# First attention: the cosine products of the rotation move from GpSimd to VectorE

## The reference

```python
qkv = x @ w_qkv.T                      # 16 query heads, 4 key heads, 4 value heads of 128, and a gate
q = _layernorm(q, q_norm_w, q_norm_b)  # over the 128 numbers of each head
k = _layernorm(k, k_norm_w, k_norm_b)
q = _rope(q, cos, sin)                 # out = [xr*c - xi*s, xr*s + xi*c]
k = _rope(k, cos, sin)
scores = einsum('bhqd,bhkd->bhqk', q, k) / sqrt(D)
attn = softmax(where(causal, scores, -inf), axis=-1)
out = einsum('bhqk,bhkd->bhqd', attn, v)
out = out * sigmoid(gate)
return out @ w_o.T
```

## Time and profile before

| what | us |
|---|---|
| three runs: median (lowest to highest) | 868.32 (867.44 to 869.45) |
| the profiled execution, whole | 867.89 |
| its span, first to last instruction | 866.2 |
| PE busy in the span | 706.4 (82%) |
| DVE busy | 576.8 (67%) |
| ACT busy | 322.8 (37%) |
| POOL busy | 306.4 (35%) |

### The profile page before, as it was taken

How to read it: one execution, slowest core, us unless ns; L and a number is a source line. 1 busy time by engine, 2 the same in 40 slices (tenths; PEclk the granted TensorE clock), 3 DMA queues, 4 the chain that set the end, 5 groups by cost and what they waited for, 6 DMA issues and landing times.

```text
span 866.2 us, 12266 instructions
## 1 busy us (share of the span) xinstructions
PE 706.4 (82%) x4097; PEld 443.0 (51%) x4114; DVE 576.8 (67%) x1797; ACT 322.8 (37%) x880; POOL 306.4 (35%) x364
## 2 busy tenths in 40 slices
PE   4579999999999999899998859727788986949960
PEld 2345555555555555567785434424455554524540
DVE  5768888888888888634115958355788853785543
ACT  1335555555555555533002224002466553214200
POOL 2432333333332223200002352673465422236274
PEclk9779999999999999999997969877899999888995
DMA  7000000010000000000198023230000005004243
GB/s 289 0 1 35 3 1 25 1 37 0 25 1 0 1 25 1 0 1 1 63 408 293 1 74 121 81 95 21 0 2 1 2 1 220 24 2 140 83 125 91
DMA packets 18686, 49.77 MB, mean 57 GB/s; under 512 B 4032, under 2 KB 12992, under 8 KB 18112
## 3 DMA queue, kind: packets, MB, share of 16 engines
q1 hardware_dynamic: 13728, 35.75, 11.0%
q0 software_dynamic: 4896, 13.24, 5.3%
HBM read 41.32 MB, written 7.34 MB: 56 GB/s over the span
## 4 chain that ended last, share of the span: by engine, by line
PE 30%; DVE 30%; POOL 17%; issue 10%; ACT 7%; DMA 5%; POOLq 0%; SPq 0%; ACTq 0%; DVEq 0%
PE ps L1234 6%; POOL ma L465 6%; ACT nq L619 5%; POOL xg L588 4%; POOL hrs L471 4%; DVE ps L787 4%; DVE probs L929 4%; DVE prod L1110 3%; PE ps L1526 3%; DVE hst L874 3%; PE ps L1443 2%; DVE qT L885 2%; DVE oT L939 2%; PE ps L1576 2%; DMA y_rows<-turn 2%
## 5 line engine op out<-in xcount | busy, mean ns | idle before, releaser
L787 DVE CUSTOM_DVE_ANT_0 ps<-ps,maskb 128x512 f32<-128x512 f32 (+3 forms) x256 | 119.3, 518 | 64.2 <-PE ps L1255 49.0
L1220 PE MATMUL ps<-w_qkv_a,xnT 128*128 128x512 f32 (+1 forms) x256 | 98.9, 515 | 11.2 <-ACT nq L619 10.5
L471 POOL TENSOR_TENSOR hrs<-hve,half 128x5 f32<-128x5 f32 x32 | 38.6, 1206 | 159.1 <-DVE hneg L900 159.0
L654 ACT COPY pT<-ps 128x512 f32<-128x512 f32 (+1 forms) x96 | 43.2, 523 | 121.2 <-PE ps L1335 121.2
L619 ACT ACTIVATE nq<-ps,hnm,hrs 128x128 f32<-128x128 f32 x160 | 59.4, 459 | 69.2 <-POOL hnm L473 69.2
L588 POOL DMA_INDIRECT xg<-y_rows,slot_of x64 | 64.8, 1012 | 55.2 <-DMA y_rows<-turn 36.4
L465 POOL TENSOR_TENSOR ma<-nq,rotA 128x512 f32<-128x512 f32 x32 | 54.4, 1701 | 65.5 <-ACT nq L619 65.5
L1255 PE MATMUL ps<-kT,qT 128*128 128x512 f32 (+3 forms) x256 | 76.6, 443 | 1.0 <-DVE qT L885 1.0
L1267 PE MATMUL ps<-pT,vA 128*128 128x512 f32 (+3 forms) x256 | 74.2, 433 | 0.0
L635 ACT ACTIVATE probs<-ps,negmax 128x512 f32<-128x512 f32 (+3 forms) x128 | 66.6, 559 | 9.3 <-DVE negmax L787 8.7
L1172 DVE SCALAR_TENSOR_TENSOR x_res<-xg,share,x_res 128x256 f32<-128x256 f32 x64 | 31.3, 489 | 51.5 <-DMA xg<-y_rows,slot_of 49.8
(11 more groups left out here) (175 smaller groups left out, 1422.0 us busy)
## 6 DMA issues: line engine op xcount, KB each, us to landing
w_down<-in_w_down SPq DMA_DIRECT2D x2, 4096.0 KB, 13.2
y_rows<-turn SPq DMA_DIRECT2D x32, 128.0 KB
w_qkv_a<-in_w_qkv SPq DMA_DIRECT2D x4, 768.0 KB, 5.1
w_gate<-in_w_gate SPq DMA_DIRECT2D x4, 512.0 KB, 3.2
w_o<-in_w_o SPq DMA_DIRECT2D x1, 2048.0 KB, 13.1
xn_rows<-xn SPq DMA_DIRECT2D x2, 1024.0 KB, 9.8
x_res<-in_x SPq DMA_DIRECT2D x2, 512.0 KB, 6.1
xg<-y_rows,slot_of POOLq DMA_INDIRECT x64, 2.8
```

Of the source, the lines that this page charges most:

```text
L471: pool.tensor_tensor(hrs[:], hve[:], half[:, 0:REP + 1], ALU.pow).then_inc(head_pow, 1)
L787: return dve.tensor_tensor_reduce(out=scores, in0=scores, in1=maskb[:, S - (i4 + 1) * P:], scale=-1.0, scalar=HUGE, op0=ALU.add, op1=ALU.m ...
L1220: mm = pe.matmul(dst, xnT[:, k, col:col + P], w, start=(k == 0), stop=(k == KT - 1))
```

## The change

The two products with the cosine table leave GpSimd's step and are written into VectorE's, between the two products with the sine table and the addition. They keep their shapes, their operands and their semaphore. GpSimd keeps the power and the product behind it. The order of GpSimd's instructions alone had kept it from overwriting `hrs` and `hnm` before ScalarE had read them; now a wait on `norm_done` in front of the power does.

```diff
@@ pool, step @@
-                if 1 <= r <= TILES:
-
-                    n = (r - 1) % ST
-                    pool.wait_ge(norm_done, s * (REP + 1))
-                    if r >= 2:
-                        pool.wait_ge(rope_done, s - 1)
-                    pool.tensor_tensor(ma[:, 0:REP], nq[:, 0:REP], rotA[:, 0, n:n + 1].broadcast_to([P, REP, HD]),
-                                       ALU.mult).then_inc(rotA_done, 1)
-                    pool.tensor_tensor(ma[:, REP], nq[:, REP], rotA[:, 1, n], ALU.mult).then_inc(rotA_done, 1)
                 if r < TILES:
 
                     pool.wait_ge(st_done, 2 * (s + 1))
+                    if r >= 1:
+                        pool.wait_ge(norm_done, s * (REP + 1))
                     pool.tensor_tensor(hrs[:], hve[:], half[:, 0:REP + 1], ALU.pow).then_inc(head_pow, 1)
@@ dve, step, rotated @@
                     dve.tensor_tensor(plain(mb[:, REP:J]), swapped(nq[:, REP:J]), plain(rotB[:, 1, n:n + 1]),
                                       ALU.mult).then_inc(rotB_done, 1)
+                    if r >= 2:
+                        dve.wait_ge(rope_done, s - 1)
+                    dve.tensor_tensor(ma[:, 0:REP], nq[:, 0:REP], rotA[:, 0, n:n + 1].broadcast_to([P, REP, HD]),
+                                      ALU.mult).then_inc(rotA_done, 1)
+                    dve.tensor_tensor(ma[:, REP], nq[:, REP], rotA[:, 1, n], ALU.mult).then_inc(rotA_done, 1)
                     dve.wait_ge(rotA_done, s * 2)
                     dve.wait_ge(rotB_done, s * 2)
```

## The result

| kernel | runs | median us (lowest to highest) | ratio to before, 95% interval |
|---|---|---|---|
| before, beside the first comparison | 4 | 868.07 (867.44 to 869.45) | |
| with the change | 4 | 853.81 (848.92 to 856.61) | 0.9835 [0.9813, 0.9856] |
| before, beside the second comparison | 9 | 867.90 (865.80 to 870.19) | |
| with the change, again | 5 | 855.31 (854.16 to 856.68) | 0.9854 [0.9835, 0.9873] |

The change makes the kernel 14.3 us faster in the first comparison and 12.6 in the second. The forecast was 855.9, 12.4 less than before. All nine executions lie between 848.9 and 856.7.

The account below looks back on a forecast made before the run. No engine is full; a loop through VectorE, GpSimd and ScalarE sets the 11.19 us step. Full steps gain 14.0 us, the filling loses 1.6: 12.4 off the median 868.32 gives 855.9 us, range 852.5 to 860.0.

Parts of the forecast that it names:

- Full step: Steps 6 to 32: sine product to addition falls from 2.31 to 1.79 us, gaining 0.52; step 11.19 to 10.67.
- The exponentials' lid: VectorE's reciprocal also needs ScalarE's exponentials, so a full step can gain at most 0.52 to 0.55 us.
- Collision: GpSimd and VectorE, reading `nq` together, hold each other up; the small sine product is stretched by 1.08 us.
- rival (c): Small sine product slow by itself in full steps; step row 0.56 us longer, about 885 us; chance 0.03.
- 27 steps: All full steps, r = 6 to 32, at 0.52 us each: 14.0 us gained.
- Filling: Steps before r = 6: moved products are new VectorE work, 0.80 us each in steps 4 and 5; 1.6 lost.
- the up to 2 us on top: Filling steps 2 to 4: extra loss if GpSimd's power had to wait for VectorE's whole rotation.
- Rival (a): Reciprocal waits for exponentials or a dearer product, 0.10 to 0.17 us a step; about 859.5 us; chance 0.18.
- Rival (b): TensorE keeps its clock in step 32, or step 5's scores run faster; 854 us; chance 0.14.
- Rival (d): Another loop through TensorE takes over at once: nothing gained, filling paid; 870 us; chance 0.03.
- Signs of being wrong: Reciprocal waits for ScalarE, power's median rises above 1.17 us, or stages behind 369 us change their length.
- TensorE's lid: Full steps: from 0.71 us of waiting, TensorE could not do a step below 10.48 us.

Follow-up runs that it names:

- GpSimd's unread products: The changed kernel, but GpSimd still makes both cosine products every step, into a tile that no instruction reads; 893.30 us in one run.
- the late gating: The changed kernel with VectorE's gating of a head's output put behind the next tile's moments in steps 6 to 31; 842.89 us, ratio 0.9709.

## Why the prediction was right, and where it was not

- *Full step.* Forecast 10.67, measured 10.66. The three first pitches were right (0.61, 0.20, 0.60 for 0.60, 0.20, 0.60). The fourth was 0.32 and not 0.39, so the addition came at 1.73 and not 1.79. The exponentials' lid, which the forecast put at 0.52 to 0.55, took 0.05 of that back, and 0.53 was left. That the two nearly cancel is luck; that no more than 0.55 could come out was read rightly from the earlier trace rows, and leaving out a product showed that it is a lid.
- *Collision.* The reading of the 1.36 us as GpSimd's doing was an inference from step 5. GpSimd's unread products showed it, and with it rival (c) fell: the small product is not slow by itself. Moving the small product alone showed that the stretch stays when the wait of 0.35 is gone. That both engines read the same `nq`, as the prediction put it, is not needed for it: the rows of the filling below show the like with no tile in common.
- *27 steps.* 26 distances gave 13.9 and 13.7 us and the last step half a microsecond, so 14.4 and 14.2 together: 14.0 forecast.
- *Filling.* 1.6 forecast; 1.0 and 1.7 in the two traces by the stages, 1.2 and 1.9 by GpSimd's share of it put back. The steps shared it as said: 0.74 each in 4 and 5 (the addition at 1.73 against 0.99). One part of the mechanism was not foreseen: not the power but the small product behind it is held, for the whole addition. GpSimd's row begins 0.06 behind VectorE's and ends 0.06 behind its end:

```profile
36.15 1.53 POOL L464 TENSOR_TENSOR hrs<-hve,half 128x5 f32<-128x5 f32 x1 [7.16 <-DVE hneg L898]
...
36.58 0.29 DVE L855 TENSOR_TENSOR mb<-nq,rotB 128x128 f32<-128x128 f32 x1
36.78 0.68 DVE L859 TENSOR_TENSOR ma<-nq,rotA 128x512 f32<-128x512 f32 x1
...
37.39 0.28 DVE L861 TENSOR_TENSOR ma<-nq,rotA 128x128 f32<-128x128 f32 x1
...
37.70 0.82 DVE L864 TENSOR_TENSOR mb<-ma,mb 128x640 f32<-128x640 f32 x1
37.76 0.82 POOL L466 TENSOR_TENSOR hnm<-hneg,hrs 128x5 f32<-128x5 f32 x1
```

  It takes 0.20 in a full step. The power is 1.53 to 1.54 as it was the earlier trace rows, 0.37 longer than in a full step: that is less than the length of one large product of VectorE's, and not the run of them, and the up to 2 us on top did not come. The other way round nothing was held: VectorE's three products beside the power are 0.29, 0.68 and 0.28 long, as in a full step. What the Trainium skill ("SBUF — State Buffer", section "Who interferes with whom") says against the change is thus half borne out: GpSimd's small product waits for VectorE's addition, but the power, though it began first, did not keep VectorE's products out for its 1.53; here the measurement decides.
- *Rival (a)* was half there: the exponentials are the later half of the tie, but by 0.05 (0.79 for 0.74 from the addition to the reciprocal) and not by 0.10 to 0.17. *Rival (b)* came true in one trace and not in the other; two traces do not show whether the change makes it likelier. *Rival (d)* fell by the step.
- *Signs of being wrong.* In the full steps the reciprocal's line shows no idle time before it; its 4 waits of 4.6 us in all lie behind step 32 and were there before (4.7 us). The power's median is 1.17 as before. The stages behind the last gating changed by 3.9 us in the first trace, most of it by the clock of the router's projection, and by 0.1 in the second.
- *TensorE's lid.* This step failed. From 0.71 us of waiting I concluded that TensorE cannot do a step below 10.48. It does one in 10.25. The row of a group of matmuls is longer than the distance from its start to what follows it without a wait. Here is the projection ahead of the transposes, 1.88 long before the change and with the late gating; first before:

```profile
191.00 1.88 PE L1220 MATMUL ps<-w_qkv_a,xnT 128*128 128x512 f32 x4
```

  Then with the late gating:

```profile
193.44 1.88 PE L1222 MATMUL ps<-w_qkv_a,xnT 128*128 128x512 f32 x4
...
195.16 0.60 PE L1284 MATMUL ps<-ident,mb 128*128 128x128 f32 x4
```

  With the late gating the transposes start 1.72 behind it. Before, they started 2.59 behind it (193.59 in the earlier trace rows), so TensorE lost 0.87 there and not 0.71: idle time that a view shows is a lower bound of the slack. That gives 11.19 - 0.87 = 10.32; most of the rest is the transposes themselves, with 0.55 to the next projection with the late gating and 0.60 before. In the forecast the error cost nothing, since the exponentials ended the gain first; in the expectation for the late gating it was some 7 us (850 for 842.9).
- *GpSimd's busy time* fell by 63.7 us and not by some 70. The products were 70.6 (54.4 and 16.2); 1.9 came back in the held small products, 4.3 in products of the shared expert, which are longer in this one trace (25.0 us; 20.7 before and 20.3 in the second trace).
- *Behind the rotation* the forecast expected the clock of step 32 to fall; it did so in the second trace. The median of the nine executions, 854.5, is 1.4 under the forecast. Where these 1.4 lie is open, since only two of the nine have a trace: the fastest, which gained 6.0 us behind step 32, where its clock stayed up, and one of 856.1, which gained 0.5 there.

## What to carry to other kernels

Where an elementwise product is split over GpSimd and VectorE and both read SBUF at the same time, look at the longest of each engine's instances beside the shortest: a 128x128 product that takes 1.36 us here and 0.28 there may be paying for its neighbour, and giving all of it to VectorE can be faster than sharing. Then ask what ends last next: here the gain stopped at the exponentials, and a product that was taken away besides brought nothing. Before trusting an engine's idle time as its lid, measure the distance from start to start where nothing waits, or move something off the loop and see. Work that belongs to neither end of a loop is worth trying elsewhere: the gating, moved, gave another 0.41 us a step (10.66 to 10.25).

## What the runs showed of the hardware that I had not expected

- A GpSimd product of 128x5, 0.20 us by itself, was 0.82 long behind a VectorE addition of 128x640 with two SBUF inputs that had begun 0.06 earlier: it ended only 0.06 behind it.
- The collision goes both ways in turns: with two products on each engine, GpSimd's became 1.78 and 0.50 (1.26 and 0.46 alone), VectorE's 1.36 and 0.94 (0.28 and 0.68 alone).
- After the same idle times TensorE's clock fell in one execution and not in another (2.40 against 1.31 us for ten transposes). The Trainium skill, "TensorE: Matmul & The Clock Gate", section "What's actually happening", says of the start of a kernel that the number of matmuls at the lower level varies between runs of the same kernel; these two traces show the like in the middle of one.
